# Graph network, passes 3 and 4: every seventh pair of edge groups built on the tensor engine instead of every tenth, and five extra pairs instead of six

## The chip, the cores and the metric

The kernel runs on one core of a Trainium2 chip. The metric is the device time of one execution in microseconds; lower is better. The five engines are PE (matrix multiply), DVE (vector), ACT (scalar, activations), POOL (here it issues the indirect gathers) and SP (here it issues the large transfers).

## The reference, cut to what matters

Four graph layers follow one another on a graph of 6250 nodes and 106250 edges, sorted by target. The change touches the last layer, a relational convolution that is applied twice (passes 3 and 4):

```python
def _rgcn_conv(x, src, dst, edge_type, edge_weight, W, root, bias):
    xj = x[src]
    m = jnp.zeros((xj.shape[0], W.shape[2]), dtype=x.dtype)
    for r in range(W.shape[0]):
        mask = (edge_type == r).astype(x.dtype)[:, None]
        m = m + mask * (xj @ W[r])
    m = m * edge_weight[:, None]
    out = jax.ops.segment_sum(m, dst, num_segments=x.shape[0])
    return out + x @ root + bias
...
h = jax.nn.relu(_rgcn_conv(x, src, dst, edge_type, ew, W1, root1, b1))
h = _rgcn_conv(h, src, dst, edge_type, ew, W2, root2, b2)
```

So pass 3 sums, for every target node, the weighted and relation-transformed rows of its source nodes, and pass 4 does the same with the result of pass 3. Source, target, relation and weight of an edge are the same in both passes.

## The kernel before

The padded edges are 208 groups of 512, or 104 pairs of groups (`PAIRS`). Each of passes 3 and 4 (`late_pe`, `late_dve`, `late_act`, `late3_sp`, `late4_sp`) is a loop of 104 turns, one for each pair `h`, and every engine has its own copy of it, written out without loops. A pair is done in one of two ways.

**A gathered pair.** The product of every node with the four relation matrices lies in a table in HBM (`table_rel`). POOL fetches the rows of 1024 edges with eight indirect DMAs (L660), into one of four buffers (`LATE`). ACT makes the weighted one-hot matrices of the targets, 128 x 72 each (L2709 and L2714), one-hot buffers also four. PE multiplies the two (`pair_half`, L1715, two halves a turn), and DVE adds the 128 x 72 sum to the accumulator at the place of the pair (L1495).

**A built pair.** No row is fetched. A matrix with a row for every node and a column for every (relation, target) is built, multiplied with the node features, and the result with the relation matrices. The matrix is made in ten units for each pair: two groups by five ranges of ten node tiles. `unit_codes` on DVE (L1575) compares codes to make four one-hot matrices of 128 x 440; `half_lo` (L1555) makes the twelve other factors for each five units; `unit_fill` on PE (L1728) makes four tiles of 128 x 440 from three matmuls each, in two calls of two tiles, in two banks in turn; `put_unit` on DVE clears the unit's buffer beyond the first 11 columns (MEMSET L1648), copies tile 0 from its bank (L1638) and adds tiles 1 to 3 at their offsets (L1640), which frees the banks again. `unit_use` on PE (L1764) multiplies the finished unit with ten tiles of the node features, 144 columns each (4 relations by `GW` = 36). After five units `unit_take` copies the sum out (L1626), and in the pair's own turn eight short matmuls (L1686) take the place of the pair's halves.

Two buffers `late_a` (one in `work`, one in `w_both`) hold units k and k+1, k % 2 picks one. `put_unit(k)` waits for the use of unit k-2 and for its store. In pass 3, SP stores each unit to HBM (`kept`, 720 KB); in pass 4 the stored units of the same pairs are loaded back (`late4_sp`), so that there only `unit_use` is left. Pass 4 also builds pairs of its own, the extra pairs (`X_PAIRS`: 17, 32, ... 92; `extra_fill` L1739, `extra_use` L1749, MEMSET L1600, one buffer `x_a` only, which the next unit's clearing waits for).

The pairs and turns are fixed by numbers. `PERIOD = 10` gives the built pairs 10, 20, ... 100, ten pairs or 100 units. `UNIT_AT` gives one unit to each turn: unit k is used in turn k, and `BUILD_AT` has it filled one turn earlier. PE's turn of pass 3 runs: `unit_fill` of the next unit, tiles 0 and 1; first half of the pair; node work; `unit_fill`, tiles 2 and 3; second half; `unit_use`. PE takes its queue in order. The calls differ in what they wait for: `unit_fill` of tile 2 waits until tile 0 is copied out, that of the next unit's tile 0 until tile 2 is added.

**Node work.** Each 256 nodes that are complete are worked on in between, 25 blocks in 104 turns: in pass 3 the root product (L2400), the products with the relation matrices for the next table (L2402, L2419), transposes (L2422, L2751) and the next root product (L2758). Pass 4 starts when the table is stored.

## Time and profile before

| | us |
|---|---|
| median of 3 runs (lowest to highest) | 3844.39 (3841.83 to 3845.22) |
| profiled execution, its own time | 3840.92 |
| span of the profiled execution | 3838.9 |
| PE busy / PE weight loads busy | 3455.1 / 2961.8 |
| DVE / ACT / POOL busy | 2470.5 / 2042.3 / 2647.7 |
| pass 3, first to last gather | 1990.55 to 2930.5 |
| pass 4, first to last gather | 2946.32 to 3827.2 |

The span is cut into stages by the times at which POOL's gathers from a new table begin. Within a stage, what matters is which engine never waits. In the views below a row of matmuls gives the start, the time from the first start to the last end, and the number of instructions; an f32 matmul is two instructions, and the end of the last is modelled, so the start of the next row tells better when PE was free. "Idle before" stands in square brackets with what ended it.

### The profile page before, as it was taken

The page shows a single profiled execution, that of the slowest core. Times are in us where ns is not written, and L with a number is a line of the kernel's source. Part 1 is how long each engine was busy: PE and PEld are TensorE (multiplying, and loading weights), DVE is VectorE, ACT ScalarE, POOL GpSimd, SP SyncE. Part 2 cuts the span into 40 slices and gives each one's busy share as a digit, 9 for nine tenths or more (in the row PEclk, how much of TensorE's full clock was granted, in tenths as well). Part 3 has the DMA queues.
Part 4 walks back from the last instruction along what each step waited for, and adds up shares of the span by engine and source line. Part 5 has one row for each costly group of instructions (what it writes and reads, how often), then busy time and mean ns, then how long its engine had stood idle before and what let it go on. Part 6 is the DMA issues. An engine that isn't in the chain of part 4 may idle for free. (4 is left out here: it accounts for less than half of the span.)

```text
span 3838.9 us, 70907 instructions
## 1 busy us (share of the span) xinstructions
PE 3455.1 (90%) x23412; PEld 2961.8 (77%) x23412; DVE 2470.5 (64%) x7952; ACT 2042.3 (53%) x4808; POOL 2647.7 (69%) x2736
## 2 busy tenths in 40 slices
PE   6999999999999999699978888888886899999995
PEld 5999888998887888588856666676665778888885
DVE  6999998998976555766666665666562354444431
ACT  4555555555546555556565555555555444544453
POOL 5777777777752666365547777777776777777776
PEclk8999999999999999799989999999997999999997
DMA  7666666666675666466634444444443444444453
GB/s 232 191 190 191 187 190 182 189 193 188 186 214 129 157 160 158 112 161 171 171 102 149 145 151 146 149 149 154 143 154 100 132 142 150 150 141 144 148 157 91
DMA packets 438499, 609.19 MB, mean 159 GB/s; under 512 B 266274, under 2 KB 310818, under 8 KB 437987
## 3 DMA queue, kind: packets, MB, share of 16 engines
q1 hardware_dynamic: 310162, 342.89, 28.6%
q0 software_dynamic: 100624, 234.79, 23.5%
q10 hardware_dynamic: 27330, 26.78, 2.3%
q8 instruction: 193, 3.16, 0.3%
q14 instruction: 190, 1.56, 0.1%
HBM read 451.89 MB, written 152.35 MB: 157 GB/s over the span
## 5 line engine op out<-in xcount | busy, mean ns | idle before, releaser
L660 POOL DMA_INDIRECT work<-table_rel,reli x1454 | 1378.2, 948 | 488.7 <-issue 435.6
L660 POOL DMA_INDIRECT work<-table_pre,srci x831 | 815.5, 981 | 263.2 <-issue 259.6
L2709 ACT ACTIVATE work<-iota,local 128x72 f32<-128x72 f32 x1456 | 376.4, 341 | 456.4 <-PE bank L1715 452.0
L1715 PEld LDWEIGHTS bank<-work 128*128 128x128 f32 x2912 | 392.6, 203 | 231.6 <-DMA work<-table_rel,reli 213.8
L1715 PE MATMUL bank<-work 128*128 128x72 f32 x2912 | 405.6, 285 | 163.6 <-DMA work<-table_rel,reli 162.9
L2714 ACT ACTIVATE work<-work,ew,src_both 128x72 f32<-128x72 f32 x1456 | 512.1, 434 | 6.1
L1416 PE MATMUL bank<-counts,piece_hi 128*128 128x468 f32 x1176 | 462.0, 393 | 17.2 <-issue 9.6
L1044 ACT ACTIVATE X<-bank 128x468 uint8<-128x468 f32 (+1 forms) x624 | 327.8, 544 | 280.9 <-PE bank L986 276.4
L947 PE MATMUL bank<-w_both,work 128*128 128x256 f32 x1664 | 433.7, 386 | 18.3 <-DVE work L881 9.8
L1416 PE MATMUL bank<-counts,piece_lo 128*128 128x468 f32 x1176 | 448.0, 381 | 0.0
L959 PE MATMUL bank<-work 128*128 128x64 f32 x3328 | 400.5, 274 | 3.7 <-DVE hist L828 2.9
L959 PEld LDWEIGHTS bank<-work 128*128 128x128 f32 x3328 | 395.5, 193 | 9.1 <-issue 6.0
L1051 ACT ACTIVATE work<-work 128x512 f32<-128x512 f32 x416 | 252.9, 629 | 166.2 <-DVE work L881 165.0
L881 DVE TENSOR_TENSOR work<-work,bank 128x512 f32<-128x512 f32 x416 | 266.6, 679 | 92.8 <-DMA work<-table_pre,srci 84.1
L660 POOL DMA_INDIRECT work<-table_mean,srci x207 | 210.0, 1015 | 168.1 <-PE bank L1402 87.4
L947 PEld LDWEIGHTS bank<-w_both,work 128*128 128x128 f32 x1664 | 290.3, 192 | 44.5 <-issue 10.1
L660 POOL DMA_INDIRECT work<-table_gcn,srci x207 | 209.4, 1012 | 119.8 <-PE bank L1402 59.8
L1640 DVE TENSOR_TENSOR work<-work,bank 128x440 f32 x330 | 202.4, 613 | 106.7 <-PE bank L1728 43.9
L1416 PEld LDWEIGHTS bank<-counts,piece_hi 128*128 128x128 f32 x1176 | 227.2, 193 | 50.7 <-issue 14.9
L986 PE MATMUL bank<-X 128*128 128x234 bf16 (+3 forms) x2080 | 259.6, 251 | 7.0 <-ACT X L1044 6.9
L1728 PE MATMUL bank<-work,late_lo 128*128 128x440 bf16 x1050 | 236.9, 356 | 31.0 <-DVE work L1575 14.1
L1416 PEld LDWEIGHTS bank<-counts,piece_lo 128*128 128x128 f32 x1176 | 227.0, 193 | 29.9 <-issue 2.4
(335 smaller groups left out, 6022.0 us busy)
## 6 DMA issues: line engine op xcount, KB each, us to landing
work<-ea_cols SPq DMA_DIRECT2D x208, 256.0 KB, 2.9
kept<-work SPq DMA_DIRECT2D x50, 720.0 KB
kept<-w_both SPq DMA_DIRECT2D x50, 720.0 KB
work<-kept SPq DMA_DIRECT2D x50, 720.0 KB
w_both<-kept SPq DMA_DIRECT2D x50, 720.0 KB
adj<-X SPq DMA_DIRECT2D x156, 225.0 KB
work<-adj SPq DMA_DIRECT2D x60, 585.0 KB
work<-table_rel,reli POOLq DMA_INDIRECT x1454
```

Of the source, the lines that this page charges most:

```text
L660: pool.indirect_dma_start(into[:, u, :], None, tables[p], bass.IndirectOffsetOnAxis(ap=idx_of(p)[:, t:t + 1].bitcast(U32), axis=0)).then_i ...
L881: dve.tensor_tensor(g, g, bank[q % 2 * 2 + h][:, :], ALU.add).then_inc(pre_added, 1)
L947: mm = pe.matmul(bank[q % 2 * 2 + h][:, j * HID:(j + 1) * HID], ea[:, slot, u * P:(u + 1) * P], w1a[:, 1, :], start=True, stop=True)
L959: pe.matmul(into[:, c * WIN:(c + 1) * WIN], gat0[:, q % SLOTS0, u, c * F:(c + 1) * F], hot0[:, hq, u, 0:WIN], start=(u == 0), stop=(u == U ...
L986: mm = pe.matmul(into[:, :, A_OFF[u]:A_OFF[u] + w], hot_lo[q % HOTS][:, u, :], code[:, j % A_CODES, at:at + (hi - lo) * w].rearrange("p (h ...
L1044: act.activation(stage[:, j % A_STAGES, lo * AW:hi * AW], bank[A_BANKS_AT[b % 2]][:, 0:(hi - lo) * AW], ACT.Copy).then_inc(a_taken, 1)
L1051: act.activation(pairs, pairs, ACT.Relu).then_inc(done, 1)
L1416: mm = pe.matmul(bank[D_BANKS[step % 2]][:, 0:D * AW], x[:, i * CT + t, :], counts[n % 2][:, t, :], start=(i * CT + t == BLANK and x is pi ...
L1715: mm = pe.matmul(bank[4 + m % LATE_BANKS][:, 0:PAIR_WIN], late_gat[n % LATE][:, u, :], late_hot[:, n % LATE_HOTS, u * PAIR_WIN:(u + 1) * P ...
L1728: mm = pe.matmul(bank[A_BANKS_AT[u % 2]][:, 0:RHI * CW], late_lo[:, n // RANGES % 2, u * PIECES + i, :], late_code[n % 2 * U + u], start=( ...
L2709: ins = act.activation(hot3[:, u, :], iota[:, 0:PAIR_WIN], ACT.Abs, bias=local[:, t:t + 1], scale=-1.0)
L2714: ins = act.activation(hot3[:, u, :], hot3[:, u, :], ACT.Relu, bias=ew[:, t:t + 1], scale=src_lo[:, t:t + 1])
```

## The change

`PERIOD` becomes 7: the built pairs are 7, 14, ... 98, fourteen pairs or 140 units. A period of seven turns has ten units, given to turns by `TURN`: turns 0, 2 and 4 of a period use two units, the others one, and each unit is filled in the turn before its use. So the turns before those fill two. `USED_AT` lists the units of a turn, and the loops of PE, DVE and SP go over lists instead of single units. On PE, where two units are used, the first use stands before the next unit's tiles 2 and 3; where two are filled, the one use and the second unit's tiles 0 and 1 stand behind the first unit's tiles 2 and 3, and its tiles 2 and 3 at the end. The columns per relation `GW` go from 36 to 37. The extra pairs of pass 4 are 22, 40, ... 94, five instead of six (`X_EVERY` 18 instead of 15, so that ten units spread over 18 turns). Three small arrays change place.

```diff
--- before.py
+++ after.py
@@ -77,7 +77,7 @@
 LIMIT = [min(GROUPS, int(PER_BLOCK * (k + 1) + PLAN)) for k in range(BLKS)]
 RING = 4
 LATE, LATE_HOTS, LATE_BANKS, LATE_LAG, NODE_LAG = 4, 4, 2, 2, 5
-PERIOD = 10
+PERIOD = 7
 D_PAIRS = range(PERIOD, PAIRS, PERIOD)
 G_PAIRS = [h for h in range(PAIRS) if h not in D_PAIRS]
 TW = 11
@@ -85,13 +85,14 @@
 RANGES = 5
 RHI = NT // RANGES
 CW = RELS * TW
-GW = 36
+GW = 37
 GC = RELS * GW
 PIECES = 3
 D_UNITS = len(D_PAIRS) * 2 * RANGES
 TAKES = D_UNITS * U + D_UNITS // RANGES
-UNIT_AT = {PERIOD * (k // (2 * RANGES)) + k % (2 * RANGES): k for k in range(D_UNITS + 1)}
-BUILD_AT = {h - 1: k for h, k in UNIT_AT.items()}
+TURN = (0, 0, 1, 2, 2, 3, 4, 4, 5, 6)
+TURNS_OF = [PERIOD * (k // len(TURN)) + TURN[k % len(TURN)] for k in range(D_UNITS + 1)]
+USED_AT = {h: [k for k in range(D_UNITS + 1) if TURNS_OF[k] == h] for h in range(-1, PAIRS + 6)}
 PRIME_PAIR = 4
 PADDED = TILES - -(-E // P)
 EARLY = 2
@@ -99,7 +100,7 @@
 SPREADS = 3
 INV_AT = LIMIT[-(-FIRST_CHUNKS * CH // BLK) - 1] + LAG + EAS + 7
 AGG_AT = {next(g for g in range(GROUPS + SLOTS) if g % SLOTS == SLOTS - 1 and g > LIMIT[k]): k for k in range(BLKS)}
-X_EVERY, X_FIRST, X_N = 15, 17, 6
+X_EVERY, X_FIRST, X_N = 18, 22, 5
 X_PAIRS = range(X_FIRST, PAIRS, X_EVERY)
 X_COLS = len(X_PAIRS) * PU
 X_UNITS = len(X_PAIRS) * 2 * RANGES
@@ -259,7 +260,7 @@
         late_iota = src_hi[:, CODE:2 * CODE].bitcast(FP16)
         d_code = src_hi[:, 2 * CODE:2 * CODE + D_COLS]
         d_lo = b2b_row[:, 0:D_COLS]
-        d_w = [b1a_row[:, i * D_COLS:(i + 1) * D_COLS] for i in range(PIECES)]
+        d_w = [b1a_row[:, i * D_COLS:(i + 1) * D_COLS] for i in range(PIECES - 1)]
         d_sum = more[:, 0:2 * GC].rearrange("p (o c) -> p o c", o=2)
         d_first = count[:, 0:D_COLS]
         kept = nc.dram_tensor("kept", [D_UNITS, P, RHI * GC], F32).ap()
@@ -274,7 +275,9 @@
         x_first = count[:, D_COLS:D_COLS + X_COLS]
         x_at = 2 * CODE + D_COLS
         x_codes, *x_w = (src_hi[:, x_at + i * X_COLS:x_at + (i + 1) * X_COLS] for i in range(1 + PIECES))
-        x_lo = b2b_row[:, D_COLS:D_COLS + X_COLS]
+        x_lo = count[:, D_COLS + X_COLS:D_COLS + 2 * X_COLS]
+        x_end = x_at + (1 + PIECES) * X_COLS
+        d_w.append(src_hi[:, x_end:x_end + D_COLS])
         staging_x = view(11280 + D_COLS, X_COLS).bitcast(I32)
 
         def in_extra(x):
@@ -1465,7 +1468,8 @@
                 extra_lo(dve, 0)
             places = {}
             if p == 3:
-                unit_codes(dve, BUILD_AT[-1])
+                for n in builds(-1):
+                    unit_codes(dve, n)
             for h in range(PAIRS + LATE_LAG):
                 if h < PAIRS and h % BASES == 0:
                     at = at + load_bases(dve, h)
@@ -1494,13 +1498,16 @@
                         there = acc[:, 0, bass.ds(at[h - LATE_LAG], PAIR_WIN)]
                         dve.tensor_tensor(there, there, into[:, 0:PAIR_WIN], ALU.add).then_inc(late_added, 1)
                     node(dve, h - LATE_LAG)
-                if p == 3 and BUILD_AT.get(h, D_UNITS) < D_UNITS:
-                    unit_codes(dve, BUILD_AT[h])
-                take_at = BUILD_AT if p == 3 else UNIT_AT
-                if h - 1 in take_at:
-                    unit_take(dve, p, take_at[h - 1])
-                if p == 3 and BUILD_AT.get(h + 1, 1) % RANGES == 0 and BUILD_AT[h + 1] < D_UNITS:
-                    half_lo(dve, BUILD_AT[h + 1] // RANGES)
+                codes_due = [k for k in builds(h) if p == 3]
+                takes_due = list(USED_AT.get(h if p == 3 else h - 1, ()))
+                while codes_due or takes_due:
+                    if codes_due and codes_due[0] - 2 not in takes_due:
+                        unit_codes(dve, codes_due.pop(0))
+                    else:
+                        unit_take(dve, p, takes_due.pop(0))
+                for k in builds(h + 1) if p == 3 else ():
+                    if k % RANGES == 0:
+                        half_lo(dve, k // RANGES)
                 if p == 4:
                     if h - 1 in X_AT:
                         extra_take(dve, X_AT[h - 1])
@@ -1609,6 +1616,12 @@
                 dve.wait_ge(x_used, k + 1)
                 dve.tensor_copy(x_sum[:, k // RANGES % 2, :], bank[X_BANK][:, 0:GC]).then_inc(x_summed, 1)
 
+        def uses(h):
+            return [k for k in USED_AT.get(h, ()) if k < D_UNITS]
+
+        def builds(h):
+            return uses(h + 1)
+
         def takes_before(p, k):
             if p == 4:
                 return TAKES_BEFORE + TAKES + k // RANGES
@@ -1660,23 +1673,24 @@
             else:
                 pe.wait_ge(rel_emptied, emptied(1, BLKS))
             if p == 3:
-                unit_fill(pe, BUILD_AT[-1], 0)
-                unit_fill(pe, BUILD_AT[-1], 2)
+                for n in builds(-1):
+                    unit_fill(pe, n, 0)
+                    unit_fill(pe, n, 2)
             for h in range(PAIRS):
                 m = (p - 3) * PAIRS + h
-                unit = UNIT_AT.get(h, D_UNITS)
-                build = BUILD_AT.get(h, D_UNITS) if p == 3 else D_UNITS
+                used = uses(h)
+                new = builds(h) if p == 3 else []
                 if p == 3 and h == PAIRS - 1:
                     node3_turn(pe, BLKS - 1)
                     node3_root(pe, BLKS - 1)
-                if build < D_UNITS:
-                    unit_fill(pe, build, 0)
+                if new:
+                    unit_fill(pe, new[0], 0)
                 if p == 4 and h in X_AT:
                     extra_fill(pe, X_AT[h], 0)
                 built = h in D_PAIRS or p == 4 and h in X_PAIRS
                 if built:
                     if h in D_PAIRS:
-                        pe.wait_ge(a_taken, sums_taken(p, unit))
+                        pe.wait_ge(a_taken, sums_taken(p, USED_AT[h][0]))
                     else:
                         pe.wait_ge(x_summed, X_PAIRS.index(h) * 2 + 2)
                     pe.wait_ge(late_added, m - LATE_BANKS + 1)
@@ -1689,16 +1703,23 @@
                 else:
                     pair_half(pe, p, h, 0)
                 node(pe, h)
-                if build < D_UNITS:
-                    unit_fill(pe, build, 2)
+                if len(used) > 1:
+                    unit_use(pe, p, used.pop(0))
+                if new:
+                    unit_fill(pe, new[0], 2)
+                if len(new) > 1:
+                    unit_use(pe, p, used.pop(0))
+                    unit_fill(pe, new[1], 0)
                 if p == 4 and h - 1 in X_AT:
                     extra_use(pe, X_AT[h - 1])
                 if p == 4 and h in X_AT:
                     extra_fill(pe, X_AT[h], 2)
                 if not built:
                     pair_half(pe, p, h, 1)
-                if unit < D_UNITS:
-                    unit_use(pe, p, unit)
+                if len(new) > 1:
+                    unit_fill(pe, new[1], 2)
+                for k in used:
+                    unit_use(pe, p, k)
             for h in range(PAIRS, PAIRS + NODE_LAG):
                 node(pe, h)
 
@@ -2458,8 +2479,7 @@
 
         def late3_sp(sp):
             for h in range(-1, PAIRS + 4):
-                k = BUILD_AT.get(h, D_UNITS)
-                if k < D_UNITS:
+                for k in builds(h):
                     sp.wait_ge(a_taken, takes_before(3, k) + U)
                     sp.sem_inc(gate, 1)
                     sp.dma_start(kept[k:k + 1, :, :].rearrange("o p c -> p (o c)"), late_a[k % 2].rearrange("p t k c -> p (t k c)")
@@ -2837,8 +2857,9 @@
             for k in range(2):
                 load(k)
             for h in range(PAIRS + 5):
-                if UNIT_AT.get(h, D_UNITS) + 2 < D_UNITS:
-                    load(UNIT_AT[h] + 2)
+                for k in uses(h):
+                    if k + 2 < D_UNITS:
+                        load(k + 2)
                 for b in due(h, 4):
                     sp.wait_ge(n2_step, (len(UNITS) + b) * 4 + 4)
                     sp.sem_inc(gate, 1)
```

Passes 3 and 4 have 90 and 85 gathered pairs after the change, 94 and 88 before.

**PE, pass 3, turns 1 and 2.** Lines: L1728 (now L1749) is `unit_fill`, three matmuls a tile; L1715 (now L1736) a half of a gathered pair; L1764 (now L1785) `unit_use`; the others node work. Before:

```order
L1728 MATMUL bank<-work,late_lo 128x440 x6
L1715 MATMUL bank<-work 128x72 x4
L2758 MATMUL bank<-work,w_both 128x256
L1728 MATMUL bank<-work,late_lo 128x440 x6
L1715 MATMUL bank<-work 128x72 x4
L1764 MATMUL bank<-w_both,X 128x144 x10
L1728 MATMUL bank<-work,late_lo 128x440 x6
L1715 MATMUL bank<-work 128x72 x4
L1728 MATMUL bank<-work,late_lo 128x440 x3
L1728 MATMUL bank<-src_both,late_lo 128x440 x3
L1715 MATMUL bank<-work 128x72 x4
L1764 MATMUL bank<-work,X 128x144 x10
```

After:

```order
L1736 MATMUL bank<-work 128x72 x4
L2778 MATMUL bank<-work,w_both 128x256
L1749 MATMUL bank<-work,late_lo 128x440 x3
L1749 MATMUL bank<-src_both,late_lo 128x440 x3
L1785 MATMUL bank<-work,X 128x148 x10
L1749 MATMUL bank<-work,late_lo 128x440 x6
L1736 MATMUL bank<-work 128x72 x4
L1749 MATMUL bank<-work,late_lo 128x440 x12
L1736 MATMUL bank<-work 128x72 x4
L1785 MATMUL bank<-w_both,X 128x148 x10
L1749 MATMUL bank<-work,late_lo 128x440 x3
L1749 MATMUL bank<-src_both,late_lo 128x440 x3
```

In the first, a use and a fill of the same turn have half a pair between them. In the second, turn 1 (ahead of the x12) fills two units around one use; in turn 2 a use is followed at once by tiles 2 and 3 of the next unit; the second half and the second use of turn 2 come behind these rows.

**DVE, pass 3, the loop's turns 1 and 2 after the change.** L1582 is `unit_codes`, L1562 `half_lo`, L1661 the MEMSET of `put_unit`, L1651 and L1653 its copy and adds, L1499 the add of a gathered pair:

```order
L1661 MEMSET work 128x40x26
L1651 COPY work<-bank 128x40x11
L1653 TENSOR_TENSOR work<-work,bank 128x40x11 x3
L1582 TENSOR_SCALAR work<-src_both 128x440 x4
L1562 TENSOR_SCALAR late_lo<-iota_b,b2b_row,b1a_row 128x128 x2
L1562 TENSOR_SCALAR late_lo<-iota_b,b2b_row,src_both 128x128
...
L1499 TENSOR_TENSOR acc<-acc,bank 128x72
L1661 MEMSET w_both 128x40x26
L1651 COPY w_both<-bank 128x40x11
L1653 TENSOR_TENSOR w_both<-w_both,bank 128x40x11 x3
```

The twelve factors of `half_lo` for the next five units now stand ahead of the MEMSET of unit 3; before the change they stood behind the adds of that unit.

## Rows read from the trace of the kernel before

**Rows 1.** Page, part 2: busy tenths, 40 slices of 96 us.
```profile
PE   6999999999999999699978888888886899999995
POOL 5777777777752666365547777777776777777776
```
**Rows 2.** Windows: pass 3 and pass 4.
```profile
core 0: us, PE busy (x) PEld busy (x) DVE busy (x) ACT busy (x) POOL busy (x), PEclk, DMA share, GB/s
2004.50:2930.50 926.00, 799.46 (x5096) 621.23 (x5096) 538.41 (x1312) 506.52 (x1599) 700.76 (x740) 0.95 0.45 147
2946.30:3827.20 880.90, 759.32 (x5554) 681.05 (x5554) 378.02 (x1032) 428.95 (x1418) 666.84 (x703) 0.95 0.47 140
```
**Rows 3.** Timeline of POOL: first and last gather of pass 3, of pass 4.
```profile
1990.55 0.94 POOL L660 DMA_INDIRECT work<-table_rel,reli  x1 [30.34 <-DMA table_rel<-work]
...
2929.59 0.94 POOL L660 DMA_INDIRECT work<-table_rel,reli  x1 [0.30 <-issue]
2946.32 0.95 POOL L660 DMA_INDIRECT work<-table_rel,reli  x1 [15.79 <-DMA table_rel<-work]
...
3826.22 0.95 POOL L660 DMA_INDIRECT work<-table_rel,reli  x1 [0.30 <-issue]
```
**Rows 4.** Timeline of PE, pass 3: four turns in which no gather is waited for.
```profile
2375.89 1.28 PE L1728 MATMUL bank<-work,late_lo 128*128 128x440 bf16 x6
2377.01 1.01 PE L1715 MATMUL bank<-work 128*128 128x72 f32 x8
...
2380.37 2.66 PE L1764 MATMUL bank<-w_both,X 128*128 128x144 f32 x20
2382.87 1.28 PE L1728 MATMUL bank<-work,late_lo 128*128 128x440 bf16 x6
...
2386.03 0.67 PE L2400 MATMUL bank<-work,w_both 128*128 128x256 f32 x2 [1.04 <-ACT work L2738]
...
2406.69 1.28 PE L1728 MATMUL bank<-work,late_lo 128*128 128x440 bf16 x6
```
**Rows 5.** Windows: the same four turns, and the five behind them.
```profile
2375.90:2406.70 30.80, 29.54 (x205) 23.30 (x203) 21.18 (x52) 19.55 (x63) 23.20 (x25) 1.00 0.50 167
2407.00:2456.00 49.00, 40.55 (x251) 30.71 (x249) 27.00 (x65) 24.23 (x77) 37.10 (x40) 0.93 0.47 152
```
**Rows 6.** Timeline of PE, start of pass 3: unit 0 ahead of turn 0.
```profile
1999.75 2.36 PE L1728 MATMUL bank<-work,late_lo 128*128 128x440 bf16 x6 [14.10 <-DVE work L1575]
...
2004.51 1.47 PE L1728 MATMUL bank<-work,late_lo 128*128 128x440 bf16 x6 [0.35 <-DVE work L1640]
```
**Rows 7.** Timeline of DVE, pass 3: one unit of the four turns, and `half_lo`.
```profile
2381.70 1.28 DVE L1575 TENSOR_SCALAR work<-src_both 128x440 bf16<-128x440 f16 x4
2383.31 0.89 DVE L1648 MEMSET w_both<- 128x1000 f32 x1 [0.33 <-PE bank L1764]
2384.24 0.62 DVE L1638 COPY w_both<-bank 128x440 f32<-128x440 f32 x1
...
2389.41 2.77 DVE L1555 TENSOR_SCALAR late_lo<-iota_b,b2b_row,b1a_row 128x128 bf16<-128x128 bf16 x12
```
**Rows 8.** Timeline of PE, pass 4: an extra unit's use, the fill behind it, the next use.
```profile
3057.43 2.70 PE L1749 MATMUL bank<-work,acc 128*128 128x144 f32 x20
3062.00 1.45 PE L1739 MATMUL bank<-work,late_lo 128*128 128x440 bf16 x6 [1.88 <-DVE work L1638]
3063.28 2.37 PE L1764 MATMUL bank<-work,acc 128*128 128x144 f32 x18
```
**Rows 9.** Groups of instructions in pass 4 (2950 to 3830): busy, mean ns, idle before.
```profile
L1715 PE MATMUL bank<-work 128*128 128x72 f32 x1401 | 193.0, 284 | 59.2 <-DMA work<-table_rel,reli 59.1
L1739 PE MATMUL bank<-work,late_lo 128*128 128x440 bf16 x714 | 162.9, 358 | 64.6 <-DVE work L1638 63.3 <-DVE work L1640 0.3
```
**Rows 10.** Timeline of PE, pass 3: a use behind a long wait.
```profile
2442.64 1.11 PE L1715 MATMUL bank<-work 128*128 128x72 f32 x8 [2.56 <-DMA work<-table_rel,reli]
2443.59 4.33 PE L1764 MATMUL bank<-work,X 128*128 128x144 f32 x20
```

## The prediction

> **What bounds the kernel now.** I read the page by stages first. In its 40 slices PE is busier than POOL in nearly all [rows 1], but a share of busy time alone says little, so the question in each stage is which engine never waits. The change touches passes 3 and 4 alone; I leave the 1990 us ahead of them as they are. In the timeline POOL's gathers of pass 3 begin at 1990.55 and the last ends at 2930.5: 940 us for 94 x 8 = 752 gathers, 1.25 us each, and a gather starts every 1.25 us without a gap. Pass 4 begins at 2946.32 and its last gather ends at 3827.2: 881 us for 88 x 8 = 704, again 1.25 [rows 3]. POOL is busy only 76% of both passes because 0.30 us behind each gather counts as idle, but it is full. So **POOL sets the pace of both passes**: 10.0 us for each gathered pair, and nothing for a built one.
>
> The second question is how much room PE has below that. Over pass 3 PE is busy 799 of 926 us [rows 2]. Better than that share is a stretch where nothing is waited for from POOL. Behind a built pair up to four gathered pairs lie ready, and PE runs at its own pace: four turns from 2375.89 to 2406.69, in 30.80 us [rows 4], with PE busy 29.54 of them, and the clock at its full level, 1.00 [rows 5]. They hold one unit each and one block's node work (there are 25 blocks for 104 turns). **PE's own turn is thus 30.80 / 4 = 7.70 us**, against POOL's ten-turn period of 90 us, 9.0 a turn. In the next five turns, PE waits for gathers and is busy only 40.55 of 49 us [rows 5]. PE's room in pass 3 is 1.3 us a turn, no more.
>
> **The change, part by part.**
>
> *POOL, pass 3.* 90 gathered pairs in place of 94: 4 x 8 x 1.25 = 40 us less, if POOL stays the bound. In pass 4, 85 in place of 88: 3 x 8 x 1.25 = 30 us less.
>
> *PE, pass 3.* 140 units in place of 100. A unit is two fills and a use: from 2375.89 to the next row at 2377.01 a fill of two tiles holds PE 1.12, and from 2380.37 to 2382.87 a use holds it 2.50 [rows 4]; together 2 x 1.12 + 2.50 = 4.74. That is on the path as soon as PE is the bound. A built pair's short matmuls cost PE about what a gathered pair's do, so that edit counts nothing. A period of seven turns has ten units and six gathered pairs: PE needs 7 x 7.70 + 3 x 4.74 = 68.1 us, POOL 6 x 10.0 = 60. **PE takes over as the bound.** Fourteen periods: 98 x 7.70 + 42 x 4.74 = 754.6 + 199.1 = 953.7. The use is 148 columns wide, not 144, 2.8% of 2.50 or 0.07 more: 140 x 0.07 = 9.8. Sum 963.5.
>
> *New waits in the double turns.* In a turn that uses two units, the use of unit k is followed at once by tiles 2 and 3 of unit k+2, which lies in the same buffer. So DVE can clear only behind that use, then copies tile 0, and only then has PE its bank. The same chain stands in pass 4, where the extra pairs have one buffer: the use starts at 3057.43, the fill behind it at 3062.00 [rows 8]; less 2.50 for the use, PE stands still 2.07 us, close to MEMSET and copy, 0.89 + 0.62 [rows 7], with their hand-overs. Nothing hides it, since PE's queue is in order: the half pair and the second use are queued behind it. Two smaller waits come with it. Tiles 2 and 3 of one unit are followed at once by tiles 0 and 1 of the next, which need the adds: about 0.5. And once in a period the factors of `half_lo`, 2.77 us on DVE [rows 7], stand ahead of a MEMSET; about 1.0 of them still fits before the use ends, and 1.77 spread over three double turns is 0.6. Against that, a longer turn hides small waits that are in the 7.70 already, about 0.3. I take 2.07 + 0.5 + 0.6 - 0.3 = 2.9 for each of 42 double turns: 121.8. The ends are 0 (all hidden) and 4.9 (the full 2.07 in the filling turn too, with 2.07 + 0.8 here): 0 to 206.
>
> *Start and tail of pass 3.* Ahead of turn 0, two units are filled, not one. The one took from 1999.75 to 2004.51 [rows 6], so turn 0 moves from 2004.5 to 2009.3. Turn 98 begins at 2009.3 + 963.5 + 121.8 = 3094.6. Four gathered pairs lie ready; the last one needs the buffer of pair 99, which is free after two turns without a unit, 2 x (7.70 - 4.74) = 5.9, and then takes 10.0. The last gather ends at 3110.5, against 2930.5: **pass 3 gets 180 us longer.** The stretch to pass 4 (15.8 [rows 3]) stays.
>
> *DVE, ACT, SP.* DVE needs 1.28 + 0.89 + 0.62 + 3 x 0.61 and gaps of 0.2, about 5.2 for a unit, and 0.55 for its share of factors, so 57.5 in a period of about 77; it is no bound by itself, its order is what counts. ACT has four pairs' hots less. A unit's store of now 740 KB must land before the buffer's next clearing, some 8 us later at the least; DMA is busy 0.45 of pass 3 [rows 2]. If that cover were gone, the MEMSET would wait.
>
> *Pass 4.* PE's side: in it gathers are waited for 59.2 us and the copy of an extra tile 63.3 us [rows 9]. The other 881 - 59.2 = 821.7 is PE's own. To it come 40 uses of 2.57, 102.8, and 0.07 for 150 uses that were there, 10.5. Ten extra units less take 47.4 off. And the chain of [rows 8] needs two extra units in adjacent turns: that is so for 5 of ten at 15 turns a pair, 30 in all, but for 2 of ten at 18, 10 in all, so 20 x 1.88 = 37.6 go. Sum 850.0. Waits for gathers that no order removes (the first turns, and the last six pairs, which have no extra work beside them) are about 30, so 880 against 881: **pass 4 -1 us**. Bounds: -30, if POOL stays the bound, and +28, if every wait stays.
>
> **Sum.** 3840.9 (own time of the profiled execution, span 3838.9) + 180 - 1 = 4019.9, or 4020. The median of the runs is 3.5 above the profiled execution; I put 4021.
>
> The clock: behind a wait of 2.56 us the next use took 4.33 us in place of 2.66 [rows 10], so it ran partly at 1.2 and not 2.4 GHz; behind one of 1.88 it took 2.37 for nine tenths of the work [rows 8], full rate. The granted clock is 0.95 over pass 3 now [rows 2], but 1.00 where PE is full [rows 5]. With waits of 2 us in full turns I take 1.00, and 0.95 as the other end. The Trainium skill (TensorE: Matmul & The Clock Gate, HAM oscillation) says that idle gaps of PE bring its slow clock back and that the first work behind pays for it; the trace agrees in the rows named. By that rule the new waits cost more than themselves, and the time would be 4075 in place of 4021.
>
> **Rivals.**
> 1. *POOL stays the bound, and it gets faster.* Place: passes 3 and 4. Price: 40 + 30 = 70 us, so 3841 - 70 + 3.5 = 3774. It decides if PE's turn with one unit is at most (60 - 3 x 4.81) / 7 = 6.5 us. For it: POOL never pauses now [rows 3]. Against it: four full turns of 7.70, with 96% busy [rows 4, 5]. In a sentence of its own: the Trainium skill (Perfetto Trace Analysis, Identifying the Most-Contended Engine) has PE judged by the busy share of its weight loads, not of its matmuls; here that is 621 of 926 us, 67%, below POOL's 76% [rows 2], and by that rule this rival would be the forecast. Chance 0.03.
> 2. *PE is the bound, but the new waits are hidden* by DVE's working ahead. 4021 - 122 = 3899. Against it: the buffer forbids working ahead. Chance 0.13, of which 0.02 with a turn of PE so much shorter that the time comes out near 3844.
> 3. *PE and DVE hand over at each tile*, so that the waits come to 4.9 a double turn: 4021 + 84 = 4105. Chance 0.12.
> 4. *The clock stays at 0.95* over a pass 3 of 1085 us: + 54, 4075. For it: today's mean. Chance 0.10.
>
> **How the numbers follow.** The forecast as it stands has 0.62. Range: 3895 to 4090 holds the forecast, rivals 2 and 4 and part of 3. A difference under 0.2%, 8 us, can hardly be told from none. Faster 0.03 (rival 1), same 0.02 (within rival 2), slower 0.95.
>
> **What would show it.** Right: gathers of pass 3 from 1990 to about 3110, POOL with gaps that end by PE's L1736; PE over 90% busy in pass 3, waits for gathers there near zero; a wait of about 2 us in each double turn ahead of L1749, ended by L1651; turns at 10.9 us on average; pass 4 near 880. Wrong: gathers every 1.25 us through pass 3 (rival 1); fills that follow a use without a gap (rival 2); waits for L1653 that sum up to more than those for L1651 (rival 3); a granted clock of 0.95 or less in a full pass 3 (rival 4).

## The result and the profile after

The changed kernel takes **4034.2 us**, median of 4 runs (4029.5 to 4037.4), against 3844.8 for the kernel before: a ratio of 1.0493, 95% interval 1.0475 to 1.0511. The forecast was 4021. The profiled execution of the changed kernel took 4037.39 us with a span of 4035.6, 196.7 more than before.

The page's busy tenths and the granted clock, to set beside [rows 1]:

```profile
PE   7999999999999997999788888888888799999996
...
POOL 5777777777716663655475555565555677777776
PEclk8999999999999997999899999999999899999997
```

What is to be seen is POOL, which falls from 7 to 5 in the slices of pass 3 and comes back in pass 4. The windows of the two passes (as in [rows 2]):

```profile
2010.30:3117.00 1106.70, 966.29 (x6167) 739.75 (x6167) 725.74 (x1753) 462.00 (x1461) 644.58 (x680) 0.97 0.43 146
3150.00:4024.00 874.00, 805.99 (x6055) 743.20 (x6054) 340.01 (x952) 421.50 (x1390) 642.99 (x679) 0.96 0.57 178
```

And POOL's timeline, first and last gather of each pass, for [rows 3]:

```profile
1989.11 1.02 POOL L663 DMA_INDIRECT work<-table_rel,reli  x1 [30.30 <-DMA table_rel<-work]
...
3143.39 0.95 POOL L663 DMA_INDIRECT work<-table_rel,reli  x1 [0.30 <-issue]
3162.13 0.95 POOL L663 DMA_INDIRECT work<-table_rel,reli  x1 [17.80 <-DMA table_rel<-work]
...
4023.00 0.94 POOL L663 DMA_INDIRECT work<-table_rel,reli  x1 [0.30 <-issue]
```

From these rows, first gather's start to last gather's end: **pass 3 is 1155.2 us long in place of 940.0, +215.2; pass 4 is 861.8 in place of 880.9, -19.1**; the stretch between is 2.0 longer, the start 1.4 earlier. The sum is the 196.7.

The groups of instructions in pass 3 (2010 to 3130), where POOL and PE wait:

```profile
L663 POOL DMA_INDIRECT work<-table_rel,reli x692 | 655.9, 948 | 465.7 <-PE bank L1736 275.2 <-issue 190.5
L1749 PE MATMUL bank<-work,late_lo 128*128 128x440 bf16 x1443 | 331.3, 353 | 125.1 <-DVE work L1651 63.1 <-DVE w_both L1651 55.5 <-DVE w_both L1653 2.7
L1736 PE MATMUL bank<-work 128*128 128x72 f32 x1367 | 179.4, 276 | 0.0
```

POOL, which never waited before, stands 275 us for buffers that PE has not read. PE never waits for a gather (0.0), and stands 125 us ahead of fills. In pass 4 (3150 to 4030) both waits of [rows 9] are smaller, 36.4 for 59.2 and 20.3 for 63.3:

```profile
L1736 PE MATMUL bank<-work 128*128 128x72 f32 x1376 | 184.6, 280 | 36.4 <-DMA work<-table_rel,reli 36.4
L1760 PE MATMUL bank<-work,late_lo 128*128 128x440 bf16 x600 | 132.7, 353 | 24.8 <-DVE work L1651 20.3 <-DVE work L1595 4.1
```

A double turn of pass 3 on PE's timeline: the use of one unit, the wait, the fill that writes for the unit in the same buffer.

```profile
2544.70 2.68 PE L1785 MATMUL bank<-work,X 128*128 128x148 f32 x20
2549.30 1.45 PE L1749 MATMUL bank<-work,late_lo 128*128 128x440 bf16 x6 [1.92 <-DVE work L1651]
2550.59 1.01 PE L1736 MATMUL bank<-work 128*128 128x72 f32 x8
2551.43 2.73 PE L1785 MATMUL bank<-w_both,X 128*128 128x148 f32 x20
```

The same moment on DVE (lines left out are the rest of the factors and codes):

```profile
2547.67 0.93 DVE L1661 MEMSET work<- 128x1040 f32 x1 [3.75 <-PE bank L1785]
2548.63 0.62 DVE L1651 COPY work<-bank 128x440 f32<-128x440 f32 x1
2549.35 2.06 DVE L1653 TENSOR_TENSOR work<-work,bank 128x440 f32 x3
2551.32 0.53 DVE L1562 TENSOR_SCALAR late_lo<-iota_b,b2b_row,b1a_row 128x128 bf16<-128x128 bf16 x2
...
2555.37 0.93 DVE L1661 MEMSET w_both<- 128x1040 f32 x1 [0.16 <-issue]
...
2562.15 0.93 DVE L1661 MEMSET work<- 128x1040 f32 x1 [1.80 <-PE bank L1785]
```

The predicted wait is there, 1.92 us. Counted over pass 3 it stands behind a use exactly 42 times, once for each double turn, 80.6 us in all. But the second MEMSET waits for nobody (0.16, issue): from 2547.67 on DVE has some 12.7 us of work without a pause, then it stands 1.80 for PE's next use. The two engines take turns in being late. That was not in the forecast, and the experiments turn on it: they ask what of the added time is PE's work, what is standing, and what is the clock.

### The profile page after: what moved, and what is told of

Its sections match the earlier page's. It is cut to its first block, busy times and chain, and to the rows that moved or that the text cites. A ratio compares the mean times of both kernels' runs of the same rounds, so it can differ in the third digit from the quotient of the medians.

```text
span 4035.6 us, 75017 instructions
## 1 busy us (share of the span) xinstructions
PE 3694.0 (92%) x25144; PEld 3162.1 (78%) x25144; DVE 2624.1 (65%) x8315; ACT 2006.2 (50%) x4696; POOL 2595.7 (64%) x2680
## 4 chain that ended last, share of the span: by engine, by line
PE 29%; DVE 10%; issue 8%; POOL 2%; DMA 1%; ACT 1%; DVEq 1%; POOLq 0%; ACTq 0%; SPq 0%
PE bank L1785 12%; PE bank L1749 5%; PE bank L1736 5%; PE bank L1770 2%; PE bank L1760 2%; POOL work L663 2%; DVE work L1582 2%; DVE late_lo L1562 1%; DVE work L1661 1%; DVE w_both L1661 1%; DVE work L1651 1%; PE bank L1700 1%; DVE work L1653 1%; DVE w_both L1653 1%; DVE w_both L1651 1%
## 5 line engine op out<-in xcount | busy, mean ns | idle before, releaser
L663 POOL DMA_INDIRECT work<-table_rel,reli x1398 | 1324.6, 947 | 740.6 <-issue 394.6
L2729 ACT ACTIVATE work<-iota,local 128x72 f32<-128x72 f32 x1400 | 361.7, 341 | 548.7 <-PE bank L1736 535.2
L2734 ACT ACTIVATE work<-work,ew,src_both 128x72 f32<-128x72 f32 x1400 | 492.4, 434 | 5.8
L1749 PE MATMUL bank<-work,late_lo 128*128 128x440 bf16 x1470 | 339.2, 354 | 142.0 <-DVE work L1651 63.4
L1736 PEld LDWEIGHTS bank<-work 128*128 128x128 f32 x2800 | 379.3, 201 | 65.9 <-DMA work<-table_rel,reli 41.5
L1736 PE MATMUL bank<-work 128*128 128x72 f32 x2800 | 374.2, 280 | 36.4 <-DMA work<-table_rel,reli 36.4
L962 PEld LDWEIGHTS bank<-work 128*128 128x128 f32 x3328 | 394.1, 193 | 12.2 <-issue 9.0
L1749 PEld LDWEIGHTS bank<-work,late_lo 128*128 128x128 bf16 x1470 | 123.1, 98 | 299.3 <-DVE work L1651 75.4
L1653 DVE TENSOR_TENSOR work<-work,bank 128x440 f32 x360 | 220.9, 613 | 131.3 <-PE bank L1760 79.3
```

What stands on the lines that cost most here:

```text
L663: pool.indirect_dma_start(into[:, u, :], None, tables[p], bass.IndirectOffsetOnAxis(ap=idx_of(p)[:, t:t + 1].bitcast(U32), axis=0)).then_i ...
L962: pe.matmul(into[:, c * WIN:(c + 1) * WIN], gat0[:, q % SLOTS0, u, c * F:(c + 1) * F], hot0[:, hq, u, 0:WIN], start=(u == 0), stop=(u == U ...
L1653: return dve.tensor_tensor(there, there, tile, ALU.add)
L1736: mm = pe.matmul(bank[4 + m % LATE_BANKS][:, 0:PAIR_WIN], late_gat[n % LATE][:, u, :], late_hot[:, n % LATE_HOTS, u * PAIR_WIN:(u + 1) * P ...
L1749: mm = pe.matmul(bank[A_BANKS_AT[u % 2]][:, 0:RHI * CW], late_lo[:, n // RANGES % 2, u * PIECES + i, :], late_code[n % 2 * U + u], start=( ...
L2729: ins = act.activation(hot3[:, u, :], iota[:, 0:PAIR_WIN], ACT.Abs, bias=local[:, t:t + 1], scale=-1.0)
```

## Experiments

Each run is given with its median and, where it decides, with the length of pass 3 and pass 4, first gather to end of last, from its trace. A table behind the runs splits pass 3 of each into the time in which PE is busy and the time in which it stands. The kernel before gave 3840.8, 3842.3 and 3840.7 us beside the three groups of runs.

**Is it PE's work? The third matmul of each tile left out.**

```diff
-                for i in range(PIECES):
+                for i in range(PIECES - 1):
...
-                                   late_code[n % 2 * U + u], start=(i == 0), stop=(i == PIECES - 1))
+                                   late_code[n % 2 * U + u], start=(i == 0), stop=(i == PIECES - 2))
```

(in `unit_fill`, of the changed kernel).

> The changed kernel, but the third of the three matmuls of each tile in unit_fill and extra_fill is left out (the lowest piece of the edge weight is missing from the built matrices); DVE's work is the same. Theory (PE's queue in order sets pass 3): the 140 units lose 4 matmuls each, 560 x 0.187 = 105 us, all of it from pass 3, and in pass 4 50 x 4 x 0.187 = 37, of which a part. Time about 3915, between 3895 and 3930. Rival (DVE's handing over of tiles sets pass 3): the fill is shorter but the next still waits for the copy and the adds, so pass 3 loses under 40 us and the waits for L1653 and L1651 grow by the rest; time above 3980.

Measured 4040.9 us, 1.053 of before (1.0511 to 1.0548); pass 3 1161.3 us, pass 4 856.5. **Nothing was gained**, so the first account fell. (The cut was made in `unit_fill` alone, not in `extra_fill` too, so for pass 4 nothing was to be expected.) The largest group of fills in this run, 2010 to 3100, to set beside the 125.1 us above:

```profile
L1749 PE MATMUL bank<-work,late_lo 128*128 128x440 bf16 x942 | 244.6, 359 | 176.8 <-DVE w_both L1651 77.6 <-DVE work L1651 69.5 <-DVE work L1653 16.9
```

and the window of pass 3, with a granted clock of 0.94 where it was 0.97:

```profile
2012.00:3125.00 1113.00, 904.09 (x5620) 711.93 (x5619) 727.18 (x1753) 461.92 (x1461) 643.84 (x680) 0.94 0.43 145
```

Over the whole pass the waits of the fills for the copy and the adds go from 121 to 191 us. The 105 us of matmuls went two ways: PE stands 69 us longer, and its busy time fell by 63 us only. A part of the missing 42 us is the slower clock: the short matmuls of a built pair took 347 ns on average where they took 284 in the changed kernel, those of a use in `work` 308 for 296. Another part are the waits themselves: in the rows above, a fill behind a wait holds PE 1.29 us until the next row (2549.30 to 2550.59), where one without a wait took 1.12 [rows 4], and there are more of them now. The two parts were not told apart.

**The same cut in the kernel before.**

> The same cut in the kernel before (third matmul of each tile left out). Theory (POOL sets both passes there): pass 3 keeps its 940 us from first to last gather although PE has 75 us less to do, pass 4 its 881; time within 5 us of 3844. Rival (PE is already a bound of its own before the change, in both passes): pass 3 shorter by over 20 us.

(Again in `unit_fill` alone, so this run speaks of pass 3 only.) Measured 3839.8 us, ratio 1.000 (0.999 to 1.001); pass 3 939.2, pass 4 879.9. POOL sets pass 3 before the change, as the forecast had it.

**One call moved: the first use of a double turn to its start.**

```diff
+                if len(used) > 1:
+                    unit_use(pe, p, used.pop(0))
                 if new:
                     unit_fill(pe, new[0], 0)
...
                 node(pe, h)
-                if len(used) > 1:
-                    unit_use(pe, p, used.pop(0))
```

> The changed kernel with one call moved on PE: in turns that use two units the first use stands at the start of the turn, ahead of the next unit's tiles 0 and 1, so that clearing and copying run beside that fill and half a pair. Same work on all engines. Theory: the wait of 1.92 us behind the use goes, and with it the small wait between two fills that now have a use between them, 42 x (1.92 + 0.3) = 93 us; PE needs 68 us for seven turns and stays the bound above POOL's 60. Time 3941, between 3925 and 3965; pass 3 about 1060 us to its last gather, POOL still with gaps. Rival (the hand-over between DVE and PE is the bound, whatever the order): the waits come back at the adds, under 30 us gained.

Measured 3920.0 us, 1.0212 (1.0193 to 1.0231); pass 3 1035.0, pass 4 864.9. 114 us gained with no work taken out. In pass 3, which is 120 us shorter, PE stands 77 us less, which is under the 93 of the theory; the other 43 are busy time, the same matmuls at a faster clock and with fewer fills behind a wait. The waits ahead of fills in the groups of 2012 to 2990:

```profile
L1749 PE MATMUL bank<-work,late_lo 128*128 128x440 bf16 x1435 | 319.3, 351 | 51.6 <-DVE w_both L1651 40.1 <-DVE work L1651 10.1
```

and the window of pass 3, with a granted clock of 0.99:

```profile
2011.00:3000.00 989.00, 926.21 (x6202) 730.52 (x6201) 728.09 (x1756) 463.55 (x1465) 645.09 (x683) 0.99 0.48 164
```

The double turns' order, with what it does to the clock, is thus worth 114 of the 190 us, the largest part of the loss.

**The extra pairs alone, in the kernel before.**

```diff
-X_EVERY, X_FIRST, X_N = 15, 17, 6
+X_EVERY, X_FIRST, X_N = 18, 21, 5
```

> The kernel before with the extra pairs of the change alone: five instead of six, ten units over 18 turns instead of 15 (pairs 21, 39, ... 93, since 40 is a built pair there). Pass 4 has 89 gathered pairs, one more than before. Theory (POOL sets pass 4 of the kernel before): one pair more, +10 us, 3854, though the waits for the copy of an extra tile fall from 63 to under 30 us. Rival (PE sets pass 4): ten units of 4.74 us and 20 waits of 1.88 less, 85 us of PE, so the time falls by more than 10 us.

Measured 3848.9 us, 1.0025 (1.0016 to 1.0035), pass 4 888.7 us for 89 pairs of 10.0. One gathered pair more, 8 us more, although PE is busy 23 us less: POOL set pass 4 before the change.

**A small clear.** After the first run the theory was a ring through both engines: PE uses a unit, DVE clears its buffer and copies tile 0, PE fills, and so on to the next use, each waiting for the other. This kernel clears one column of each relation instead of 26. Old sums stay in the built matrices, so it is a kernel for its time alone.

```diff
-            done(dve, dve.memset(late_a[k % 2][:, :, :, TW:], 0.0))
+            done(dve, dve.memset(late_a[k % 2][:, :, :, TW:GW if k < 2 else TW + 1], 0.0))
```

> The changed kernel, but put_unit clears one column of each relation instead of 26 (the two buffers are cleared once in full, so old sums stay in the built matrices). The MEMSET takes about 0.15 us instead of 0.93; PE's work is the same. Since a cut of PE's matmuls gained nothing, the theory is now a ring through both engines: use of a unit, clear, copy, then fill, half pair, next use; it is passed twice in two turns with three units, once with 1.92 us of standing and once with about 1.0. It expects 42 x 2 x 0.78 = 66 us less, and a better clock on top, 20: 3950, between 3935 and 3975. Rival (my first account: PE's own work and one wait of 1.92 in each double turn): 42 x 0.78 = 33 less, 4001. Second rival (PE's work alone): no change.

Measured 3930.3 us, 1.0224 (1.0209 to 1.024); pass 3 1046.2. The MEMSET among the groups of 2012 to 2990 (one of its two buffers):

```profile
L1661 DVE MEMSET w_both<- 128x40 f32 (+1 forms) x68 | 7.1, 104 | 58.7 <-PE bank L1785 58.4 <-issue 0.2
```

(the other buffer's took 92 ns), and the window of pass 3, where PE is busy 92% and its clock at 1.00:

```profile
2012.00:3030.00 1018.00, 939.95 (x6288) 729.41 (x6288) 620.49 (x1775) 474.18 (x1502) 657.27 (x697) 1.00 0.47 162
```

Pass 3 is 109 us shorter. That is close to what is taken from DVE (0.82 us for each of 140 units, 115), and one could read it as every unit's clear lying on the path. The split of PE's time does not bear that out. PE stands 65 us less, which is the 66 of the expectation (84 clears on the path). Its own matmuls, the same ones, take 44 us less, where the expectation had 20 for the clock; fills behind a wait are not fewer here (106 for 94), so the clock is what is left to explain it. **Work taken from DVE gave time back twice, as shorter waits and as a faster PE.**

**Use first, and the third matmul out.** (The two diffs above together.)

> The kernel with the first use at the start of a double turn, and in addition the third matmul of each tile left out, as before. In that order PE stands little, so either PE's work is the bound now, and 105 us of it in pass 3 go, down to POOL's 900 us: 3815 to 3830. Or DVE's take of a tile every 0.82 us (0.61 and the hand-over) sets the fills there too, and most of the cut turns into waits: 3880 to 3920. The theory of the ring expects the second, about 3890.

Measured 3910.2 us, 1.0171 (1.0155 to 1.0187); pass 3 1026.1 in place of 1035.0. Even in the better order 105 us of matmuls are worth 9. PE's busy time fell by 65 and its standing grew by 56. The granted clock is 0.95 from 2012 to 2990, where it was 0.99, so a part of the missing 40 us of busy time went back through the clock.

**Copy before clear.** DVE has the same work, but frees PE's bank earlier.

```diff
-            done(dve, dve.memset(late_a[k % 2][:, :, :, TW:], 0.0))
             for u in range(U):
...
                 put_tile(dve, late_a[k % 2], u, d_places).then_inc(a_taken, 1)
+                if not u:
+                    done(dve, dve.memset(late_a[k % 2][:, :, :, TW:], 0.0))
```

> The changed kernel with put_unit's order on DVE changed: tile 0 is copied first, then the other 26 columns are cleared, then the adds. Same work on both engines; PE's bank is free 0.96 us earlier, the unit is finished no earlier. Theory of the ring, in which the small clear gained 104 us: what that run took off was partly the bank's lateness (which this order takes off as well) and partly the lateness of the finished unit (which it does not). The wait of 1.92 us in each double turn becomes about 1.0: 42 x 0.93 = 39 us, and somewhat from a better clock: 3985, between 3960 and 4000. Rival (only the end of the take counts): no change, 4034. Rival (only the bank counts): the full 104, 3930.

Measured 4020.5 us, 1.047 (1.0454 to 1.0486); pass 3 1138.1, 17 us less: a miss, nearer to the rival in which the end of the take counts. PE even stands 14 us more than in the changed kernel; the gain is its busy time, 31 us less at a clock of 1.00 (2012 to 3100), though more fills stand behind a wait. The rows show why nothing came of the order itself:

```profile
2553.50 0.72 PE L1750 MATMUL bank<-work,late_lo 128*128 128x440 bf16 x3
2554.70 0.73 PE L1750 MATMUL bank<-work,late_lo 128*128 128x440 bf16 x3 [0.48 <-DVE work L1653]
...
2560.03 0.73 PE L1750 MATMUL bank<-work,late_lo 128*128 128x440 bf16 x3
2561.87 0.73 PE L1750 MATMUL bank<-src_both,late_lo 128*128 128x440 bf16 x3 [1.11 <-DVE w_both L1653]
```

(the first row of each two is tile 2, the second tile 3; line numbers are one higher.) Tile 2 can start earlier, but tile 3 needs the first add, which now stands behind the clear. The wait has moved from the copy to the add.

**Both orders together.**

> Both orders changed, period 7: first use at the start of a double turn, and copy before clear. From the run with the use first (3920), whose waits for the copy are 50 us in pass 3: theory: most of these go, 3885, between 3865 and 3905. If DVE's own row of work is the bound by then (busy 74% of pass 3, with a hand-over behind each add), nothing is gained: 3920.

Measured 3927.7 us, 1.0225 (1.0209 to 1.024); pass 3 1048.6, that is 14 us longer than with the use first alone. A miss: the copy's order gives nothing and even loses there; PE stands 21 us more.

**Other periods, with the use first.** Every ninth pair, extra pairs as before the change (`PERIOD = 9`, `TURN = (0, 0, 1, 2, 3, 4, 5, 6, 7, 8)`, 15, 17, 6):

> Built pairs every ninth (11 pairs, 110 units, one turn of nine with two units, its first use at the start of the turn), the extra pairs of the kernel before (six, every 15). POOL fetches one pair less in each pass, 93 and 87. PE needs 9 x 7.70 + 4.81 + about 1 = 75 us for nine turns, POOL 80. If POOL stays the bound in both passes the time is 3841 - 20 = 3821; PE's 26 us of uses more in pass 4 may eat 5 to 10 of it. Expected 3825, between 3818 and 3836. Rival (any double turn costs more than it gains): 3841 or above.

Measured 3849.9 us, 1.0016 (1.0007 to 1.0025), a miss by 25 us. Pass 3 took 931.4 us, POOL's floor; pass 4 892.2, 11 more than before, not 10 less: POOL waits 34.3 us there for PE, and PE 62.4 for the copy of an extra tile, as before the change. In pass 4 six extra pairs and the added uses together are too much for PE.

Every eighth pair, five extra pairs over 18 turns (`PERIOD = 8`, `TURN = (0, 0, 1, 2, 3, 4, 4, 5, 6, 7)`, 18, 21, 5):

> Built pairs every eighth (12 pairs, 120 units, two turns of eight with two units, first use at the start), five extra pairs (21, 39, ... 93). POOL fetches 92 and 87 pairs, 20 and 10 us less. PE needs 8 x 7.70 + 2 x 4.81 + about 2 = 73.2 us for eight turns, POOL 70, so PE is just the bound in pass 3: 96 turns end at 2887, and the last gather at about 2923, 8 us earlier than before; pass 4 10 us less. Expected 3823, between 3812 and 3840. Rival (the ring costs more than 2 us for eight turns): 3840 or above.

Measured 3833.1 us, 0.9973 (0.9961 to 0.9984); pass 3 939.5, pass 4 868.4: within the range, and 0.3% faster than the kernel before, all of it in pass 4. The four runs of this group began pass 3 near 1998 in their profiles where all others began at 1989 to 1993. Those runs were on another chip, and their code for the passes before is that of the changed kernel. So I compare lengths of passes; why it is so stays open.

The same with copy before clear, in `extra_take` too:

> Period 8 with the first use at the start, five extra pairs, and copy before clear in put_unit and extra_take. Pass 3 of the run without the copy order took 947 us to its last gather, 50 us of waits for the copy among them; POOL's floor is 920. Theory: pass 3 20 us shorter, pass 4 at POOL's 870 as it was: 3813, between 3805 and 3825. Rival (the end of the take counts, not the bank): 3833.

Measured **3826.6 us, 0.9964 (0.9951 to 0.9978)**, the fastest here, but its pass 3 is 936.9, only 2.6 less than without, and pass 4 870.1. The further gain expected of the copy's order did not come, and the run is a miss by its range (3805 to 3825); the 6.5 us between the two medians lie mostly ahead of pass 3, across two chips.

Six extra pairs every 14 turns in that kernel (`X_EVERY, X_FIRST, X_N = 14, 21, 6`):

> The kernel of e10_period8_copy with six extra pairs (21, 35, ... 91, every 14), so that pass 4 fetches 86 pairs instead of 87. POOL 10 us less, PE 47 us more; PE waited 68 us for gathers in pass 4 of the period 8 run, 20 of them at its end. Expected 3806, between 3798 and 3822. Rival (PE becomes the bound of pass 4): 3815 or above, that is no better than e10.

Measured 3910.4 us, 1.0181 (1.0167 to 1.0195), a clear miss; pass 4 took 952.2. In its groups of pass 4 (2950 to 3890):

```profile
L663 POOL DMA_INDIRECT work<-table_rel,reli x678 | 641.3, 946 | 300.0 <-issue 191.2 <-PE bank L1738 108.8
L1762 PE MATMUL bank<-work,late_lo 128*128 128x440 bf16 x720 | 163.6, 351 | 71.1 <-DVE work L1654 45.5 <-DVE work L1652 25.6
```

POOL waits 109 us for PE. In pass 4 PE is busy 53 us more than in the run with five extra pairs and the same order of copy and clear (817.0 for 764.0) and stands 29 us more. Ten units in 14 turns have their next unit in the adjacent turn six times of ten, so 36 times the one buffer `x_a` stands between use and fill; with 18 turns it is twice of ten, 10 times. How the loss divides between more work and this buffer was not tested. By its code this kernel lacks something more: with 14 turns to a pair, DVE writes the first sum of the next extra pair into `x_sum` in the very turn in which PE reads the sum of the pair itself, and nothing holds it back. Its values can't be relied on, and it stands here for its time alone.

**What became of PE's time in pass 3.** Windows from 20 us behind the first gather to the end of the last one, us:

| kernel | stretch | PE busy | PE stands | granted clock |
|---|---|---|---|---|
| changed kernel | 1135.2 | 990.4 | 144.8 | 0.97 |
| third matmul out | 1141.3 | 927.7 | 213.7 | 0.94 |
| use first | 1015.0 | 947.3 | 67.6 | 0.99 |
| small clear | 1026.2 | 946.2 | 80.0 | 0.99 |
| use first, third matmul out | 1006.1 | 882.6 | 123.5 | 0.95 |
| copy first | 1118.1 | 959.0 | 159.2 | 0.99 |
| both orders | 1028.6 | 940.4 | 88.2 | 0.99 |

All but the two with the third matmul out have the same matmuls to do, 6312 to 6321 of them in these windows. Their busy time still ranges from 940 to 959 us at a clock of 0.99, and is 990 at 0.97.

## Why the prediction was right, and where it was not

**POOL sets both passes before the change.** Shown: in pass 3 taking matmuls out changed nothing (1.000), and in pass 4 one pair more cost 8 us.

**POOL loses that place in pass 3.** Shown by its 275 us of waits. The rival in which it stays the bound (3774) is out. The rule of the Trainium skill (Perfetto Trace Analysis, Identifying the Most-Contended Engine) is not out with it. Before the change PE's weight loads, 67% of pass 3, lay below POOL's 76%, and POOL was the bound; after it they are 740 of 1107 us, again 67%, and above POOL's 645. What the share of before could not tell is how much of PE's room the change would take.

**A wait of about 2 us in each double turn.** Right in place and size: 1.92 us, 42 times, ended by the copy. The term as a whole, 121.8 us, was met by 121.3 us of waits for the copy and the adds, and part of that is luck: the waits for the adds, put at 21 us, came to 2.7, while waits for the copy in other places came to 38.

**The sum from turn 0 to turn 98.** It was 963.5 + 121.8 = 1085.3 us, against 1117.7 measured (2008.37 to 3126.10), 32 short. By its own rows (29.54 busy in 30.80) the sum holds 933 us of busy time and 153 of standing; measured are 977 and 141. **So the term that was mis-sized is the clock**, taken as 1.00 and measured as 0.97. In the run with the small clear, with the same matmuls, about as many waits and a clock of 0.99, PE is busy 44 us less, as much as the sum is short of. A small part of it may be the fills behind waits, 0.17 us each. The lower standing gave 12 us back. Rival 4 had the right mechanism, with a price of 54 for a clock of 0.95.

**"PE takes over as the bound", 3 x 4.74 of it for added units.** As an account of where PE's time went this is borne out. As a statement of what sets the time it is not: it would make pass 3 shorter by the 105 us of matmuls that were taken out, and pass 3 stayed (1161 and 1155); with the use first it fell by 9. Two things took the 105 us: PE stood longer (69 and 56), and the rest of its work took longer (42 and 40), by the slower clock and the fills behind waits. What the runs fit is a ring: use, clear, copy, adds, next use, with two buffers, and DVE's tasks for the next unit in its own queue in between. What is taken from PE's side of it comes back as waits for DVE, and what is taken from DVE's side shortens them (by 65 us of 115). How the 7.70 us of the four full turns, in which PE was busy 96%, divide in this way was not measured. The sentence that DVE "is no bound by itself, its order is what counts" was half right: DVE is busy only 66% of pass 3, and yet work taken from it is time gained.

**Rival 3 (hand-over at each tile, 4105)** did not come: by its own sign the waits for L1653 would exceed those for L1651, and they are 3 us against 119. Even with the third matmul out they are 41 against 150.

**Pass 3** thus grew by 215 us, not 180: 32 of the difference lie between turn 0 and turn 98, 2 in the tail.

**Pass 4**, -19 in place of -1. Fewer adjacent extra units: right, the waits for the copy fell by 43 us (37.6 in the sum). PE's own part was 821.7 + 28.3 = 850 in the sum and is 861.8 - 36.4 = 825.4. The 25 us lie in its busy time, which grew by 41 (759.3 to 799.9) where the sum has 66 (102.8 + 10.5 - 47.4). It is not the 40 more uses: the uses of built units grew by the 102.8 us of the sum (279.3 to 382.1). The fewer extra units and gathered pairs took off more than was put down, and the wider use cost less; how much of it is the clock, 0.96 for 0.95, is open. The two errors, +35 in pass 3 and -18 in pass 4, offset each other in part, which is luck, and the forecast missed by 13 us of 4034.

## What to carry to other kernels

A share of PE near 90% in a stretch does not show that PE's work sets the time. If its matmuls hand tiles to another engine and back, take a third of the matmuls out and look whether the time moves, and then do the same with the other engine. Split each result into PE's busy and standing time: a difference that looks like work taken out can be a faster clock in good part, as with the small clear (65 us of waits, 44 of busy time). When an order puts the use of a buffer directly ahead of work that needs this buffer again, move the use to the earliest place at which its input is ready; here that one call was worth 114 us. And trade work off the bounding engine only as far as the next ring has room: ten units for seven turns lost 190 us, ten for eight gained 9 to 14.

## What the runs showed of the chip that I had not expected

A wait of 2 us can cost more than itself, but not each time. In the turn shown above a wait of 1.92 us left the next use at 2.73 us. Behind another one in the same pass it took 3.85, that is, partly at 1.2 GHz instead of 2.4:

```profile
3106.62 1.45 PE L1749 MATMUL bank<-work,late_lo 128*128 128x440 bf16 x6 [1.92 <-DVE work L1651]
3107.91 1.58 PE L1736 MATMUL bank<-work 128*128 128x72 f32 x8
3109.28 3.85 PE L1785 MATMUL bank<-w_both,X 128*128 128x148 f32 x20
```

The Trainium skill (TensorE: Matmul & The Clock Gate, HAM oscillation) describes such slow spells behind idle gaps; the trace agrees in direction, with waits of 1 to 2 us each.

The clock did not follow the sum of the waits. With the copy first PE stands 159 us, more than the 145 of the changed kernel, and its clock is 0.99 for 0.97; but only 3 of its waits are of 1.5 us or more, where the changed kernel has 52 (use first 14, small clear 7). And less work can lower the clock enough to eat part of the saving: with a third of the fill's matmuls out it went from 0.97 to 0.94, and in the better order from 0.99 to 0.95, with 70 and 33 such waits. Which of the two, fewer matmuls or the waits that follow from it, brings it down is not shown.
